# An exact recurrent start on one core: waits moved into the blocks, and four blocks instead of two in a round of TensorE's pair loop

## The reference

```
gi = x_t @ W_ih + b_ih;  gh = h @ W_hh + b_hh
r = sigmoid(i_r + h_r); z = sigmoid(i_z + h_z); n = tanh(i_n + r * h_n)
h = (1 - z) * n + z * h                      # 64 steps, D = 512, 3D = 1536 gate columns
q(v) = fp8(v / scale_row)                    # rows scaled by their largest value
t = silu(q(h) @ q(w_gate).T) * (q(h) @ q(w_up).T)   # 1408 columns, with reorderings
out = x + q(t) @ q(w_down).T
```

## Time and profile before

| what | value |
|---|---|
| three timed runs | 2873.52, 2877.41, 2880.61 us (median 2877.41) |
| profiled execution | span 2879.2 us, 1.8 us above that median |
| TensorE busy | 2562.9 us, 89% of the span |
| VectorE / ScalarE / GpSimd busy | 59% / 40% / 44% |
| HBM traffic | 101 GB/s over the span |

### The profile page before, as it was taken

How to read it: one execution, slowest core, us unless ns; L and a number is a source line. 1 busy time by engine, 2 the same in 40 slices (tenths; PEclk the granted TensorE clock), 3 DMA queues, 4 the chain that set the end, 5 groups by cost and what they waited for, 6 DMA issues and landing times. The chain is left out here.

```text
span 2879.2 us, 154632 instructions
## 1 busy us (share of the span) xinstructions
PE 2562.9 (89%) x67605; PEld 1681.0 (58%) x67605; DVE 1685.2 (59%) x3398; ACT 1140.6 (40%) x2317; POOL 1262.3 (44%) x598
## 2 busy tenths in 40 slices
PE   2088999998889999999999999999996999999995
PEld 1066777776768888887675564655642444444442
DVE  8852222225632222225646778867592888888887
ACT  1321222225632222224702333323232777777773
POOL 0255666662046666664061363622700333333334
PEclk8599999999999999999999999999998999999998
DMA  6833222224422222226554253442432223232322
GB/s 193 239 85 77 74 73 71 73 71 112 131 63 71 74 73 70 73 71 167 152 135 127 92 151 118 115 156 85 129 143 93 74 84 95 84 95 84 95 63 53
DMA packets 234843, 293.74 MB, mean 102 GB/s; under 512 B 69581, under 2 KB 194023, under 8 KB 233895
## 3 DMA queue, kind: packets, MB, share of 16 engines
q1 hardware_dynamic: 212743, 240.84, 30.6%
q10 hardware_dynamic: 18304, 36.19, 3.6%
q0 software_dynamic: 3680, 15.21, 1.9%
HBM read 231.61 MB, written 60.45 MB: 101 GB/s over the span
## 5 line engine op out<-in xcount | busy, mean ns | idle before, releaser
L1145 PE MATMUL psum<-second_shared 64*32 64x384 f16 x32768 | 1026.0, 324 | 50.2 <-issue 31.3
L1153 PE MATMUL psum<-low_w,low_hot 64*32 64x384 f16 x16384 | 756.5, 324 | 2.0 <-issue 2.0
L1372 DVE TENSOR_SCALAR second_shared<-psum 32x384 f16<-32x384 f32 x496 | 272.3, 549 | 749.1 <-PE psum L1145 741.9
L953 POOL TENSOR_TENSOR low_hot<-first_shared,sum_mask 128x1024 f16<-128x1024 f16 x256 | 499.8, 1952 | 430.1 <-DVE first_shared L1359 183.8
L1145 PEld LDWEIGHTS psum<-second_shared 64*32 64x32 f16 x32768 | 561.5, 93 | 198.0 <-issue 89.8
L947 POOL TENSOR_TENSOR second_shared<-first_shared,whole_mask 128x2048 f16<-128x2048 f16 x128 | 462.5, 3614 | 460.1 <-PE psum L1145 348.2
L1044 ACT ACTIVATE second_shared<-psum 32x384 f16<-32x384 f32 x496 | 239.8, 483 | 801.9 <-PE psum L1145 795.9
L1233 PE MATMUL psum<-low_w,low_hot 64*64 64x384 f16 x12288 | 513.7, 326 | 19.9 <-issue 13.5
L1233 PEld LDWEIGHTS psum<-low_w,low_hot 64*64 64x64 f16 x12288 | 378.3, 108 | 150.4 <-issue 18.4
L310 PE MATMUL psum<-w_x,x_cols 128*64 128x512 f32 (+1 forms) x1856 | 312.0, 495 | 9.5 <-ACT x_cols L280 9.5
L1153 PEld LDWEIGHTS psum<-low_w,low_hot 64*32 64x32 f16 x16384 | 282.5, 93 | 56.8 <-issue 3.1
(11 more groups left out here) (286 smaller groups left out, 2746.6 us busy)
## 6 DMA issues: line engine op xcount, KB each, us to landing
low_w<-w_rows SPq DMA_DIRECT2D x384, 144.0 KB
low_w<-w_rows SPq DMA_DIRECT2D x256, 120.0 KB
second_shared<-w_rows SPq DMA_DIRECT2D x1024, 24.0 KB, 1.9
x_gates<-x_out ACTq DMA_DIRECT2D x58, 384.0 KB, 2.3
xg<-x_gates SPq DMA_DIRECT2D x58, 384.0 KB, 3.2
low_w<-w_rows SPq DMA_DIRECT2D x256, 72.0 KB
low_w<-w_rows SPq DMA_DIRECT2D x384, 48.0 KB
w_rows<-quantised SPq DMA_DIRECT2D x24, 384.0 KB, 4.9
```

Of the source, the lines that this page charges most:

```text
L953: nc.gpsimd.tensor_tensor(low_hot[:, buf].rearrange("p (s k) b -> p s k b", s=SUBS), low_a[:, slot, bass.ds(c, 1), :, :].rearrange("p a s ...
L1145: last = nc.tensor.matmul(run[m][u][j * Q:(j + 1) * Q, :], whole_hot[rows[u], m, sign, kk, j % 2 * Q:(j % 2 + 1) * Q], whole_w[rows[u], m, ...
L1153: nc.tensor.matmul(run[m][u][j * Q:(j + 1) * Q, :], low_hot[rows[u], m, kk, j % 2 * Q:(j % 2 + 1) * Q], low_w[rows[u], m, at:at + UC], sta ...
L1372: last = nc.vector.tensor_scalar(whole_w[u * B:u * B + Q, m, 0, bq, :], run[m][u][bq * Q:(bq + 1) * Q, :], 1.0 / HIGH_ONE, None, ALU.mult)
```

## The change

Three edits, all in what TensorE is given to do:

- In the pair chain the waits for a block no longer stand ahead of it but inside the block before: the registers at kk = 7, the bases at kk = 9, the weights at kk = 12, the one-hots at kk = 14. Only the first block's waits stand ahead of the loop.
- The loop's body holds `PAIR_STEP` = 2 values of c, four blocks, where it held one value and two blocks. It has `PAIR_ROUNDS` = 32 / 2 - 1 = 15 rounds; the last two values of c, four blocks, are written out behind it.
- In `sum_chain` the waits of a block likewise move into the block before (kk = 11 and 13), apart from the first of each `four`; and the plain loops have 4 rounds of eight blocks in place of 8 rounds of four.

No matmul, DMA or other engine's instruction is added or removed.

```diff
--- before.py
+++ after.py
@@ -41,6 +41,7 @@
 
 BK = 16
 BUFS = 4
+PAIR_STEP = 2
 PAIR = 2
 SK = 8
 W3, WX, W1, W2, W0, W00 = range(6)
@@ -159,6 +160,7 @@
         SUBS = BK // SK
         UC = G3 // 2 // 2
         OPERANDS = 4
+        PAIR_ROUNDS = NBK // PAIR_STEP - 1
         PB = P // BK
         Q = 32
         WHOLE_KINDS = len(WHOLE_ROWS)
@@ -1164,23 +1166,49 @@
                                     if kk == BK - 1:
                                         last.then_inc(run_ok[u], 1)
 
-                            with pe.Fori(0, NBK) as c:
+                            def based(m, c):
+                                return c * 2 + (fine_no(t, m, 0) + 1)
+
+                            def w_ready(m, c):
+                                return c * LOADED + (loaded_before(stage_of(t, m), m) + LOADED)
+
+                            def whole_ready(m, c):
+                                return c * WHOLE_LOADED + (t * NBK + 1) * WHOLE_LOADED
+
+                            def hot_ready(m, c):
+                                return c * 2 + (block_no(t, m, 0) + 2)
+
+                            def one_block(m, c, follows):
+                                nm, nc_ = (1, c) if m == 0 else (0, c + 1)
+                                for kk in range(BK):
+                                    if follows and not isinstance(c, int) and kk == BK - 9:
+                                        for value in (based(nm, nc_), w_ready(nm, nc_), whole_ready(nm, nc_), hot_ready(nm, nc_)):
+                                            pe.compute_val(value)
+                                    if follows and kk == BK - 7:
+                                        pe.wait_ge(base_v[1], based(nm, 0))
+                                        pe.wait_ge(base_v[1], based(nm, nc_))
+                                        pe.wait_ge(base_a[1], based(nm, nc_))
+                                    if follows and kk == BK - 4:
+                                        pe.wait_ge(w_in[nm], w_ready(nm, 0))
+                                        pe.wait_ge(w_in[nm], w_ready(nm, nc_))
+                                        pe.wait_ge(whole_in[nm], whole_ready(nm, nc_))
+                                    if follows and kk == BK - 2:
+                                        pe.wait_ge(hot_ok, hot_ready(nm, 0))
+                                        pe.wait_ge(hot_ok, hot_ready(nm, nc_))
+                                    term(m, kk)
+
+                            pe.wait_ge(base_v[1], based(0, 0))
+                            pe.wait_ge(base_a[1], based(0, 0))
+                            pe.wait_ge(w_in[0], w_ready(0, 0))
+                            pe.wait_ge(whole_in[0], whole_ready(0, 0))
+                            pe.wait_ge(hot_ok, hot_ready(0, 0))
+                            with pe.Fori(0, PAIR_ROUNDS) as c:
+                                for i in range(PAIR_STEP):
+                                    for m in range(2):
+                                        one_block(m, c * PAIR_STEP + i if PAIR_STEP > 1 else c, True)
+                            for c in range(PAIR_ROUNDS * PAIR_STEP, NBK):
                                 for m in range(2):
-                                    based = c * 2 + (fine_no(t, m, 0) + 1)
-                                    w_ready = c * LOADED + (loaded_before(stage_of(t, m), m) + LOADED)
-                                    whole_ready = c * WHOLE_LOADED + (t * NBK + 1) * WHOLE_LOADED
-                                    hot_ready = c * 2 + (block_no(t, m, 0) + 2)
-                                    for value in (based, w_ready, whole_ready, hot_ready):
-                                        pe.compute_val(value)
-                                    for u in range(2):
-                                        pe.wait_ge(base_v[u], fine_no(t, m, 0) + 1)
-                                        pe.wait_ge(base_v[u], based)
-                                        pe.wait_ge(base_a[u], based)
-                                    pe.wait_ge(w_in[m], w_ready)
-                                    pe.wait_ge(whole_in[m], whole_ready)
-                                    pe.wait_ge(hot_ok, hot_ready)
-                                    for kk in range(BK):
-                                        term(m, kk)
+                                    one_block(m, c, m == 0 or c < NBK - 1)
 
                         def turn_pair(tile):
 
@@ -1215,17 +1243,28 @@
                         def sum_chain(t, m):
                             def four(n, ahead):
 
+                                def w_ready(j):
+                                    return n * LOADED + (loaded_before(stage_of(t, m), sum_buf(j)) + LOADED * (1 + ahead))
+
+                                def hot_ready(j):
+                                    return n * BUFS + (block_no(t, m, j) + 2 + BUFS * ahead)
+
+                                if not isinstance(n, int):
+                                    pe.compute_val(w_ready(0))
+                                    pe.compute_val(hot_ready(0))
+                                pe.wait_ge(hot_ok, block_no(t, m, 0) + 2)
+                                pe.wait_ge(w_in[sum_buf(0)], w_ready(0))
+                                pe.wait_ge(hot_ok, hot_ready(0))
                                 for j in range(BUFS):
                                     buf = sum_buf(j)
-                                    w_ready = n * LOADED + (loaded_before(stage_of(t, m), buf) + LOADED * (1 + ahead))
-                                    hot_ready = n * BUFS + (block_no(t, m, j) + 2 + BUFS * ahead)
-                                    if not isinstance(n, int):
-                                        for value in (w_ready, hot_ready):
-                                            pe.compute_val(value)
-                                    pe.wait_ge(hot_ok, block_no(t, m, 0) + 2)
-                                    pe.wait_ge(w_in[buf], w_ready)
-                                    pe.wait_ge(hot_ok, hot_ready)
                                     for kk in range(BK):
+                                        if j + 1 < BUFS and kk == BK - 5 and not isinstance(n, int):
+                                            pe.compute_val(w_ready(j + 1))
+                                            pe.compute_val(hot_ready(j + 1))
+                                        if j + 1 < BUFS and kk == BK - 3:
+                                            pe.wait_ge(hot_ok, block_no(t, m, 0) + 2)
+                                            pe.wait_ge(w_in[sum_buf(j + 1)], w_ready(j + 1))
+                                            pe.wait_ge(hot_ok, hot_ready(j + 1))
                                         for u in range(2):
                                             for half in range(2):
                                                 own = slice(u * B, (u + 1) * B)
@@ -1238,8 +1277,9 @@
                             FOURS = NBK // BUFS
                             tiles = TILES_OF.get(t, ()) if m == 1 else ()
                             if not tiles:
-                                with pe.Fori(0, FOURS) as n:
-                                    four(n, 0)
+                                with pe.Fori(0, FOURS // 2) as n:
+                                    four(n * 2, 0)
+                                    four(n * 2, 1)
                                 return
                             with pe.Fori(0, 2) as n:
                                 four(n, 0)
```

## The result

The changed kernel takes 3471.39 us (median of 4 runs, 3460.72 to 3484.72) against 2878.28: a ratio of 1.2068, 95% interval 1.2032 to 1.2104. Forecast were 3430 us, between 3290 and 3540.

The account below looks back on a forecast made before the run. TensorE, 89% busy, was taken as the bound, the second pair chain by its own stream. Terms 490 + 14 + 27 + 20 = +551 us on the profiled 2879.2 gave 3430 us, range 3290 to 3540.

Parts of the forecast that it names:

- The loop's size: Pair chains: a four-block round touches 13 fetch blocks, all refetched each round, 50.2 us against 32.7; +490 us.
- The pitch: Pair chains: fetching code takes 3.80 us per block of 256 instructions; ends 3.46 to 4.01, -132 to +81 us.
- The jump: Pair loop's jump back: target priced as a fetched block like the others, TensorE standing some 3.5 us; ends -34 to +84.
- The first round and the last four blocks: Pair chains: 6 more cold fetch blocks in each first round, +14 us; the written-out last four blocks cold, +27 us.
- The clock: TensorE at half clock after the pair loop's jump: 0.7 us a round, +20 us; ends -20 to +50.
- The moved waits: Pair blocks: weights land 7.3 us in, kk = 12 falls at 8.3 to 9.4, so 0 us behind the fetch.
- No wait on DMA second_shared inside a round: Sign in the changed profile: TensorE never waits for these weights' DMAs within a pair-loop round.
- The other signs: Changed profile: about 465 q8 packets, "issue" idle near 450 us, rounds 50 us, chains about 800 us, other stretches unchanged.
- The sum chains: Sum chains: moved waits and halved jumps give 0, first pass covered; if not, under 8 us.
- Rival 2: Pair chains: all 13 fetch blocks kept, weights' wait sets the block, +146 and some 15 us cold: 3040; chance 0.13.
- Rival 1: Pair chains: part of the loop's code is kept; if 3 blocks survive, -101 us: 3330 to 3390; chance 0.14.

Follow-up runs that it names:

- the waits at the blocks' heads: Changed kernel with its round of four blocks kept, but each block's waits put back ahead of it; 3417.35 us, ratio 1.1889.
- x = 2, 4 and 6: Kernel before with 2, 4 or 6 extra zero-weight steps of 24 matmuls in each pair block; 3406.31, 3824.23 and 4059.04 us.
- the kernel whose loop was moved: Kernel before with two zero steps a pair block, plus 54 clearing matmuls ahead of the second pair chain; 3007.74 us, ratio 1.0461.

## Why the prediction came out right

*The loop's size* was the whole case and held: 13.4 packets in a later round on the mean (489 - 68 = 421 more in all, some 400 forecast), 52.3 us a round on the mean of both chains against 50.2 + 0.7. That 13 blocks aren't kept had been argued, not read; the runs show the limit at 8 with the one asked for ahead. The Trainium skill, "Runtime: NRT & Kernel Launch", section "Instruction fetch mechanics", gives 2048 instructions for TensorE, 8 blocks of 256: the trace agrees once the block ahead is counted. The sentence of that section of the Trainium skill that crossings are mostly hidden is half right: at 5.2 us a block they are (43 packets, 7 us), at 2.6 they are not (0.66 to 1.21 us idle in the earlier trace rows; the 0.88 of the prediction is the least of the second chain).

*The pitch* of 3.80 us a block held with the waits at the blocks' heads: 50.4 us a round on the mean of both chains against 50.9, and a whole effect of +540 against the sum's +551. *The jump* was priced as a block like the others and shows 3.41 us idle, against some 3.5. *The first round and the last four blocks*: 48.8 and 47.6 us in that kernel, means of both chains, against some 46.5 forecast for each.

*The clock* behaved as the earlier trace rows had shown; behind the jump the timeline reads

```profile
1152.37 0.57 PE L1155 MATMUL psum<-low_w,low_hot 64*32 64x384 f16 x8
```

where 0.36 is the figure at 2.4 GHz, and the granted clock of the second chain is 0.93 for 1.00. The round with the waits at the blocks' heads came out 0.2 us above the 50.2 that hold no clock term, where 0.7 was forecast for it; how much of the time the clock makes by itself no run separates. In the changed kernel it costs at a second place, which is told under the moved waits.

*The moved waits* are the mis-sized term: 0 forecast behind the fetch, +54 measured. "No wait on DMA second_shared inside a round" was one of the prediction's signs, and it failed: the second chain alone has 46. I had compared when kk = 12 is reached (8.3 to 9.4 us into a block) with the landing of before (7.3). In the second chain's later rounds kk = 12 is reached after 7.5 to 8.6 us, 8.0 on the mean, and TensorE goes on after 8.9 on the mean. Three things make the cost. First, the landing is later when code is being fetched. In the changed kernel the load that starts at 1124.66 reads

```profile
1124.66 1.84 SPq L851 DMA_DIRECT2D low_w<-w_rows  x2
1126.68 1.75 SPq L858 DMA_DIRECT2D second_shared<-w_rows  x4
1128.62 1.49 SPq L851 DMA_DIRECT2D low_w<-w_rows  x2
1130.29 1.75 SPq L858 DMA_DIRECT2D second_shared<-w_rows  x4
```

Two issues take 0.79 us in the earlier trace rows and here 1.84 and 1.49; the weights are there at about 1133.4, where TensorE goes on: 8.8 us after the load's start, not 7.1.

Second, a wait that stands early in a fetch block delays the fetch of the next one. TensorE enters a block at 1127.46 and q8 has its packet between 1127.5 and 1129. It enters the next at 1131.07, reaches kk = 12 after 40 matmuls and waits until 1133.45, and q8 has nothing between 1131.1 and 1133.4; the row of 1133.4 to 1135 is

```profile
q8 instruction: 1, 0.02, 4.6%
```

and the next stop comes at 1136.9, 5.8 us behind the last one instead of 3.8. Read over that chain's 14 later rounds, this holds for every wait that stands 40 or 42 matmuls into its fetch block: in all 28 the packet comes 0.9 to 1.5 us after the wait's end and the next stop 5.1 us after the last on the mean. It doesn't hold for those that stand 44 matmuls in, nor for the first chain's, 46 to 51 in: there the packet comes 1.0 to 1.8 us after the block is entered, whether TensorE still waits or not. One such block is entered at 1195.13 and waits until 1199.11; from 1196.2 to 1197.2

```profile
q8 instruction: 1, 0.02, 8.8%
```

So the next block seems to be asked for when TensorE is some 43 matmuls into the running one. The packets a round point the same way: where the loop's last fetch block begins 46 matmuls or more before the jump (x = 2, 4 and 6), one packet more than blocks touched; where it begins 17 to 20 before it (the waits at the blocks' heads), 12.9 for 13 touched. The changed kernel, whose last one begins 13 to 20 before it, has 13.4, in between. What sets off the request wasn't tried.

Third, behind a long wait TensorE runs at half clock (1.2 GHz) for a while, which the prediction had priced for the jump alone. The wait just named, and a stretch behind it (length, busy, granted clock, DMA share, GB/s):

```profile
1199.11 0.36 PE L1147 MATMUL psum<-second_shared 64*32 64x384 f16 x8 [2.82 <-DMA second_shared<-w_rows]
```

```profile
1200.10:1202.00 1.90, 1.90 (x57) 0.50 0.03 9
```

In the later rounds of both chains 29 such waits hold TensorE for more than 2 us; the 80 matmuls behind one take 1.5 to 2.9 us, against 1.5 behind the shorter waits of the second chain, some 25 us in all, of which an unknown part is hidden in the fetch. How the 54 us divide among the three no run separates.

The page's groups put 122 us down to waits on the weights' DMAs, 16 of which the kernel before has as well ("DMA second_shared<-w_rows", two waits); the other 106 us cost 54, so about half of them was hidden after all.

*The other signs.* q8 had 489 packets where 465 were forecast, and the stretch outside the chains is as before. The idle time for "issue" is 260.1 + 85.0 = 345 us where some 450 were forecast: part of it turned into waits on the DMAs, and with the waits at the blocks' heads it is 310.9 + 123.4 = 434. A chain takes 831 and 835 us where some 800 were forecast, and 802 and 803 in that kernel.

*The sum chains*: 0 forecast, 0 measured. *Rival 2's price*, +146 and 15, was the right mechanism for two blocks in a round and 18 us short. *Rival 1's* lower figure was 3329 by its own sum and the upper one 3380, not 3390, which changes nothing.

## What to carry to other kernels

A loop on TensorE may grow only while the blocks of 256 instructions that it touches, and the next one, stay at 8: count the blocks touched, not the length, as the same 1742 instructions touched 7 or 8 by where they began, and that made 400 us in one chain. Beyond the limit every round runs at the pace of the fetch, which costs where 256 instructions take less than the fetch's 3.8 us (2.6 here) and nearly nothing where they take more. A wait may be moved ahead only as far as the trace shows the thing waited for to be ready. With two blocks in a round and the last two written out, moving three of the four kinds of wait and leaving the weights' behind the last step won 11 us, moving all four lost 179; with nothing written out the former won 22.

## What the runs showed of the hardware that I had not expected

Fetching code slows down the issue of other DMAs. Inside one kernel, the one with two zero steps, the same SP instructions were timed without fetches (first chain, first three rows: L849's and L856's durations in ns, least, median and most, and the time to landing in us) and with them (second chain):

```profile
L849 SPq DMA_DIRECT2D low_w<-w_rows x254: 287/309/431, 172.7 to 738.3; - x127
...
L856 SPq DMA_DIRECT2D second_shared<-w_rows x488: 316/372/1002, 170.9 to 732.6; - x163
DMA to landing us min/median/max: 1.6/1.8/7.1
...
L849 SPq DMA_DIRECT2D low_w<-w_rows x256: 292/309/2387, 890.4 to 1850.6; - x128
...
L856 SPq DMA_DIRECT2D second_shared<-w_rows x488: 316/372/1977, 893.4 to 1836.3; - x163
DMA to landing us min/median/max: 1.6/2.2/3.7
```

The same chain at the same place in the kernel whose loop was moved, without fetches, from 895 us on:

```profile
L849 SPq DMA_DIRECT2D low_w<-w_rows x254: 292/309/317, 897.0 to 1455.6; - x127
...
L856 SPq DMA_DIRECT2D second_shared<-w_rows x488: 316/347/592, 895.1 to 1449.0; - x163
DMA to landing us min/median/max: 1.6/1.8/2.2
```

The medians of the issues hardly move, single ones take up to 2.4 us: with fetches 101 of L856's last over 0.5 us, without them 1. In the second chain with fetches the issues that overlap a q8 packet take 0.60 (L849) and 0.80 us (L856) on the mean, the others 0.30 and 0.35; without fetches they all take 0.30 and 0.35. Longer ones overlap more easily, so the comparison of the chains is the one that counts. The landing is less clear: its median goes from 1.8 to 2.2 us here, but with six zero steps and more fetches it is 1.8 in both chains.

A loop may even touch 8 blocks and stay: in the kernel with moved waits and two blocks in a round, the second chain's first stops put its last block's start one matmul before the jump, and no later round has a packet; the same holds for the second chain with the weights' wait last. If the next block is asked for only some 43 matmuls in, the jump comes first there, and 8 blocks are all that has to stay. This is a reading of these two cases; no run was made for it.
